# Moving the feed-forward's row transposes behind the next step's query transposes, in a one-core transformer kernel

## What is computed

```python
for i in range(6):
    x = attn_layer(shift_tokens(x), Wqkv[i], q_scale[i], k_scale[i], Wo[i]) + x
    x = ffn_layer(shift_tokens(x), ln_g[i], ln_b[i], W1[i], b1[i], W2[i], b2[i]) + x

def ffn_layer(x, g, bln, W1, b1, W2, b2):
    xn = (x - mean) / sqrt(var + 1e-5) * g + bln
    a, gate = split(xn @ W1 + b1)              # 341 columns each
    return a * gelu(gate) @ W2 + b2
```

## Time and profile before

| what | value |
|---|---|
| median of 3 runs | 1494.74 us (1492.25 to 1496.88) |
| profiled execution, its own time | 1491.09 us |
| its span in the profile | 1489.3 us |
| TensorE busy (matrix) | 1436.4 us, 96% |
| VectorE busy | 1328.3 us, 89% |
| GpSimd busy | 1208.7 us, 81% |
| ScalarE busy | 1161.7 us, 78% |
| granted TensorE clock, mean | 0.989 of full |

### The profile page before, as it was taken

How to read it: one execution, slowest core, us unless ns; L and a number is a source line. 1 busy time by engine, 2 the same in 40 slices (tenths; PEclk the granted TensorE clock), 3 DMA queues, 4 the chain that set the end, 5 groups by cost and what they waited for, 6 DMA issues and landing times.

```text
span 1489.3 us, 74807 instructions
## 1 busy us (share of the span) xinstructions
PE 1436.4 (96%) x32908; PEld 784.4 (53%) x32908; DVE 1328.3 (89%) x1795; ACT 1161.7 (78%) x2288; POOL 1208.7 (81%) x1047
## 2 busy tenths in 40 slices
PE   7978999999999999999999999999999999999996
PEld 6823544555545545555555545545555555555553
DVE  5578999989999989999999999989999999999975
ACT  4337888878888888888888888888888888888882
POOL 6158999888888888888888888888888888888951
PEclk9979999999999999999999999999999999999999
DMA  6000000010000020000020000020000000000000
GB/s 209 18 14 31 3 10 11 8 62 10 3 20 15 4 66 11 3 20 16 3 67 11 4 19 16 3 66 11 3 11 24 4 10 11 3 10 25 3 11 30
DMA packets 24260, 32.67 MB, mean 22 GB/s; under 512 B 2323, under 2 KB 21120, under 8 KB 23040
## 3 DMA queue, kind: packets, MB, share of 16 engines
q1 hardware_dynamic: 23936, 27.88, 5.8%
HBM read 20.80 MB, written 1.05 MB: 15 GB/s over the span
## 4 chain that ended last, share of the span: by engine, by line
PE 90%; DVE 5%; issue 2%; POOL 1%; ACT 1%; DMA 0%; POOLq 0%; DVEq 0%; ACTq 0%
PE psq L271 23%; PE ring L293 21%; PE ring L323 11%; PE pss L312 10%; PE ring L281 9%; PE ring L337 8%; PE ring L347 4%; PE ring L370 1%; DVE qa L889 1%; PE ring L406 1%; DVE qb L905 1%; DVE qb L1024 1%; DVE mx L1046 0%; ACT sq L1277 0%; PE ring L468 0%
## 5 line engine op out<-in xcount | busy, mean ns | idle before, releaser
L293 PE MATMUL ring<-mh,x0S 128*32 128x512 f32 x3072 | 408.3, 595 | 0.0
L271 PE MATMUL psq<-wqk,x0S 128*32 128x512 f32 x3072 | 393.1, 608 | 6.8 <-ACT sq L1277 4.7
L1423 POOL TENSOR_TENSOR qa<-qa,qb 128x1024 f32<-128x1024 f32 x96 | 229.5, 2390 | 6.7 <-DVE qb L1024 6.7
L1482 POOL TENSOR_TENSOR qa<-qa,qb 128x1024 f32<-128x1024 f32 x96 | 228.4, 2379 | 0.0
L323 PEld LDWEIGHTS ring<-u,pT 128*32 128x32 f32 x6144 | 170.6, 110 | 62.3 <-issue 57.8
L1464 POOL TENSOR_TENSOR pr<-pr,rden 128x1024 f32<-128x1024 f32 x96 | 183.8, 1915 | 13.8 <-DVE rden L924 13.8
L323 PE MATMUL ring<-u,pT 128*32 128x128 f32 x6144 | 191.0, 273 | 3.6 <-ACT uT L1262 1.8
L271 PEld LDWEIGHTS psq<-wqk,x0S 128*32 128x32 f32 x3072 | 94.2, 111 | 182.8 <-issue 164.6
L1443 POOL TENSOR_TENSOR qa<-qa,rn 128x1024 f32<-128x1024 f32 x96 | 182.7, 1903 | 0.2
L1459 POOL TENSOR_TENSOR qa<-qa,rn 128x1024 f32<-128x1024 f32 x96 | 182.7, 1903 | 0.0
L312 PEld LDWEIGHTS pss<-kT,qT 64*32 64x32 f32 x12288 | 134.4, 105 | 89.7 <-issue 82.3
(11 more groups left out here) (186 smaller groups left out, 2721.2 us busy)
## 6 DMA issues: line engine op xcount, KB each, us to landing
wqk<-in_wqk SPq DMA_DIRECT2D x6, 1024.0 KB, 8.5
mvT<-in_mvT SPq DMA_DIRECT2D x6, 512.0 KB, 3.8
wo<-in_wo SPq DMA_DIRECT2D x6, 512.0 KB, 5.4
xf<-x SPq DMA_DIRECT2D x23, 128.0 KB
xf<-x SPq DMA_DIRECT2D x23, 127.0 KB
rope<-in_rope SPq DMA_DIRECT2D x1, 2048.0 KB, 10.2
w<-in_w SPq DMA_DIRECT2D x6, 341.0 KB, 2.9
xmid<-in_x SPq DMA_DIRECT2D x4, 256.0 KB, 3.8
```

Source lines behind the costliest of these rows:

```text
L271: last = mm(psq[WIN * w:WIN * w + WIN, 512 * (n % 2):512 * (n % 2) + 512], x0S[:, tile * P + WIN * w:tile * P + WIN * w + WIN], wqk[:, l % ...
L293: last = mm(bank[WIN * g:WIN * g + WIN, :], x0S[:, tile * P + WIN * w:tile * P + WIN * w + WIN], mh[:, l % 2, g, :, :].rearrange("p j n -> ...
L1423: g_.tensor_tensor(qa[:, t % 2, 1024:2048], qa[:, t % 2, 1024:2048], qb[:, 1024:2048], ALU.add).then_inc(sum_k, 1)
L1482: g_.tensor_tensor(qa[:, t % 2, 0:1024], qa[:, t % 2, 0:1024], qb[:, 0:1024], ALU.add).then_inc(sum_q, 1)
```

## The change

For the first 22 of the 24 groups the transposes `F0`, `F1` move from step `4i + 12` (behind the projection of the queries) to step `4i + 13`, directly behind `T2`, `T3` and ahead of the projection. ScalarE's two copies move one step later too, and now stand together ahead of the exponential; the second copy stood behind it. The last two groups keep their places. Sizes, counts, transfers and arithmetic are the same.

```diff
+            def rows_turned(i):
+
+                banks = [take("F0", i), take("F1", i)]
+                pe.wait_ge(xh_ready, i + 1)
+                for bank, n in banks:
+                    wait(pe, freed[bank], n)
+                halves_turned([ring[bank] for bank, n in banks], lambda blk: xh[:, blk * P:blk * P + P], QUAD)
...
                     turn([ring[bank] for bank, n in banks], t, 0)
+                i = group_at(s, 13)
+                if 0 <= i < ALLG - 2:
+                    rows_turned(i)
                 if chunk_at(s - 1, 2) >= 0:
...
                 i = feed_at(s, 12, (3, 7))
-                if i >= 0:
-                    banks = [take("F0", i), take("F1", i)]
-                    pe.wait_ge(xh_ready, i + 1)
-                    for bank, n in banks:
-                        wait(pe, freed[bank], n)
-                    halves_turned([ring[bank] for bank, n in banks], lambda blk: xh[:, blk * P:blk * P + P], QUAD)
+                if i >= ALLG - 2:
+                    rows_turned(i)
...
-                i = feed_at(s, 11, (2, 6))
+                i = feed_at(s, 12, (2, 6))
                 if i >= 0:
...
-                    for r in (0, 1) if i >= ALLG - 2 else (0,):
+                    for r in (0, 1):
...
-                i = group_at(s, 11)
-                if 0 <= i < ALLG - 2:
-                    for r in (1,):
-                        bank, n = place["F%d" % r, i]
-                        act.wait_ge(filled[bank], n + 1)
-                    l = i // GROUPS
-                    nc.scalar.activation(xnT[:, :].rearrange("p (k r n) -> p k r n", k=QUAD, r=2)[:, :, 1, :],
-                                         ring[bank][:, 0:QUAD * 64].rearrange("p (k n) -> p k n", k=QUAD), ACT.Identity, bias=par[:, l, 1:2],
-                                         scale=par[:, l, 0:1]).then_inc(freed[bank], 1)
```

## The result

The changed kernel takes 1506.08 us (median of 5 runs, 1501.94 to 1508.29), the kernel before 1492.25 us (median of 5 runs, 1490.79 to 1496.88; three of them are those of the table above). The ratio is 1.0094, with a 95% interval of 1.008 to 1.0107: the change makes the kernel 0.9% slower, 14 us. Forecast were 0.7%, 10.7 us and a time of 1505.4 us, by a wait for a PSUM bank. The profiled execution took 1508.28 us for a span of 1506.4.

A forecast was written before the change was run, and what follows sets the result against it. TensorE was taken to bound the kernel. Merging groups +3.0 us, the others +9.1 and absorbed waits -1.4 gave +10.7 us on the median of 1494.74: 1505.4 us, 0.7% slower, range 1497 to 1510.

The forecast's parts named there:

- F1's bank: Step 4i + 13: F1 gets U2's bank, so F waits 0.47 us for ScalarE's copy of U2 (line 1209).
- The price of F's new step: Step 4i + 13 grows by 0.87 us: 0.47 bank wait plus 0.40 for transposes that start alone; bounds 0.73 and 0.90.
- G0 covered by the bank wait: Step 4i + 13: the bank wait covers F's copies by 0.2 us, so G0 adds no wait.
- The exponential: ScalarE, step 4i + 13: it starts 0.74 us later behind both copies, costing nothing because of 1.21 us of idle.
- The step that loses F: Step 4i + 12: 0.54 us won with merging, only 0.17 without, where the square of the queries holds the keys' projection.
- The sum: Whole kernel: +3.0 us with merging, +9.1 without, -1.4 for pauses, together +10.7 us.
- Pauses absorb the wait: Steps 17, 33 and 65: TensorE pauses while ScalarE copies U2, so the 0.47 us wait falls away three times, -1.4 us.
- The first and the last group: Pipeline's start and end: counted like the other groups without merging; up to 1 us more allowed where the pipeline runs out.
- The rival that counted the drain alone: F's move on TensorE: nobody waits, 0.28 us won per group, 6.2 us over 22, giving 1488.5 us; chance 0.06.

The follow-up runs named there:

- Early copy and late G0: Changed kernel with ScalarE's copy of U2 ahead of the square of the keys and G0 behind the mix's second part; 1494.82 us, ratio 1.0009.
- the two runs with the early copy: Changed kernel with U2's copy ahead of the square of the keys: 1502.51 us; the same with G0 behind the mix's second part: 1494.82 us.
- that with G0 late: Changed kernel with G0 behind the second part of the mix, U2 copied where the changed kernel copies it; 1505.09 us, ratio 1.0081.
- the run with the merging groups alone: Kernel before with F moved only in 9 groups whose old step merges weights, there with U2 copied early and G0 late; 1491.7 us, ratio 0.9988.

## Why the prediction was right, point by point

- **F1's bank.** Right. The count of the ring gave U2's bank, and an idle put down to U2's copy stands in 18 groups of the changed kernel, 0.50 us in 17 of them (before the matrix instruction; the profile calls the idle of the load "issue"). The experiment that frees the bank early removes it; the one that puts F behind T3 in its old step produces it, 22 times. Forecast were 0.47 us.
- **The price of F's new step.** Forecast 0.87 us, measured 0.97. The term was undersized in two places. F's first load comes 0.11 us after the copy's end (705.18 to 705.29) and not 0.06. Then 0.43 us pass from that load to the projection's, not 0.40. The rest was in the row that the forecast started from: the projection's load came 4.74 us after T0 in step 45 and 4.71 in most steps of its kind, so TensorE is usually there 0.03 us earlier. Nothing is added behind the projection: from its load to G0's it is 2.51 us in both kernels.
- **G0 covered by the bank wait.** Right, and close: 0.2 us of cover were forecast, 0.4 were there, since the copies began 0.13 us after the start of line 1238 (the old 1231), where 0.23 were assumed, and took 1.00 us. Early copy and late G0 separate the two waits: 0.30 us of the step go with the bank alone, 0.39 more with G0's.
- **The exponential.** Right: it now starts behind both copies, at 707.65, and nothing behind it is late for that. ScalarE's idle of 1.24 us ahead of the keys' copies is still there, and the copies' order alone changes no step.
- **The step that loses F.** With merging 0.53 us were won, 0.54 forecast. Without, the mechanism was right (the square of the queries holds the projection of the keys) and the size was off: 0.08 and not 0.17 us. The early step of the earlier trace rows showed 5.31 us from line 889 to T0, and the changed kernel takes 5.40. Behind the square 0.11 us pass to the load where the early step had 0.06, which is 0.05 of the 0.09; the other 0.04 lie between that load and T0's, and why stays open. The reading that 0.06 us of room were left in the earlier trace rows was wrong: with 0.11 us behind the square, as in every such step of both kernels, the load was already held there.
- **The sum.** In the two traces the 22 steps of F are 22.4 us longer in all and the old steps 6.2 us shorter, 16.1 us net. Before the first group, where both kernels are alike, the changed one's execution was already 1.1 us later. Pauses of TensorE can explain why 16.1 is more than the runs' 14: step 49 alone is 3.76 us longer in this execution, 2.8 of them beyond the 0.97. Without these 2.8 the net is 13.3 us, against the forecast's 10.7: 22 x 0.1 us from F's step and 12 x 0.09 from the steps without merging make up the difference and a little more.
- **Pauses absorb the wait.** The forecast took -1.4 us for steps 17, 33 and 65. The number of three held, the steps did not, which is partly luck: the wait is missing in steps 17, 49 and 65, where a pause lies ahead of F, and none is recorded in step 25, which was already 0.41 us longer than its like in the kernel before. Step 33 has the wait in full, 0.51 us. How much a step grew does not show it, since the pauses themselves changed. Step 17 grew by 0.95 us without the wait, as its pauses came to 2.52 us for 1.95; step 33 grew by 0.23 with it, as its pause was 0.31 for 1.04; step 65 grew by 0.02, with 0.96 for 1.49.
- **The first and the last group.** They were counted like the others. The first won nothing in its old step (12.47 us in both kernels) and lost 1.14 in the new one. The last one's step grew by 1.37 us: the bank cost 0.26 us of waiting and G0 waited 1.05 us for the copies. The step before it shrank by the whole 0.54.

```profile
1444.97 0.47 PE L281 MATMUL ring<-ident_pad,xh 64*128 64x64 f32 x8 [0.26 <-ACT u L1216]
...
1447.51 1.07 PE L337 MATMUL ring<-xh,w 128*32 128x512 f32 x8 [1.05 <-ACT xh L1247]
```

The rival that counted the drain alone is right about its term, 0.54 us standing alone against 0.28 riding. It is wrong about the kernel: the 0.54 were mostly not there to win, for F filled a gap. The traces show what a change of shape costs: after the same T3, F's first load, of the same 64*128 form, comes 4.57 us after T0 in the two runs with the early copy, and the projection's, of the 128*32 form, 4.71 in the kernel before. The Trainium skill's rule (page TensorEngine Tiling (Array Packing), section Key Properties), that a change of tiling mode drains TensorE, agrees with these 0.14 us and did not decide the time. The prediction counted one change less per group; by the forms there are two less, into F and out of it, and 0.54 - 0.28 = 0.26 us is about twice 0.14.

## What to carry to other kernels

In a ring of banks that is handed out in program order, moving a piece of work past another changes whose copy it waits for in time: write down the last four uses at the new place and look up when each is emptied, before counting what the move saves. A stretch whose chain lies wholly on one engine can still hold work that is nearly free: what stands between two instructions tied by another engine's chain (here VectorE's rotary and ScalarE's square) fills a gap, and taking it out wins only what is above that chain. And two waits that end 0.4 us apart hide each other; removing one shows the other, so both have to be priced at once.

## What the runs showed of the hardware that was not expected

- Eight 64-row transposes add 0.28 us to the step when they follow others of their kind directly. From their first load to the next piece's it is 0.42 us then, and 0.43 us when TensorE has waited before them; what riding saves is the 0.14 us ahead of them.
- TensorE's load came 0.07 us after the end of the copies of F that it waited for (in two kernels), 0.11 us after the copy of U2, and after the square of the queries 0.11 us in the feed-forward's steps and 0.06 us in the early step of the earlier trace rows.
- TensorE pauses of 0.2 to 2.5 us with no releaser come back in steps 17, 33 and 65 of every kernel, and in step 49 of four: step 49 took 14.62 us in the kernel before, 18.37 in the changed one and 15.29 in that with G0 late. Cutting the 1 MB loads that are issued in these steps did not remove them. What causes them was not found (the packets of the instruction queue are a lead), and they limit how finely a single trace can be compared.
- Behind some of these pauses the granted clock was 0.50 (1.2 GHz) for one stretch of 3.4 us and 1.00 again after it: in step 65 of the run with the merging groups alone, from 982.9 to 986.3 us, behind a pause of 1.61 us. That step took 18.23 us, where the other kernels show 15.71 to 16.92. Behind the longest pause, 2.52 us in step 17 of the changed kernel, the granted clock stayed at 1.00.
